# The mixed part of a graph-network kernel with the next graph's preparation first, tags in the matmul weights and interleaved VectorE chains

## What is computed

```python
neigh = (adj_ > 0) & ~eye                      # 512 x 512 per graph
rank = jnp.cumsum(ni, axis=-1) - ni            # which neighbour of the row is it
nb = ni.sum(-1)
skip = where(nb > 10, (nb + 1) // 2, 1)
rem = neigh & (skip > 1) & (rank % skip == skip - 1) & mask   # neighbours that are dropped
rem = rem | swapaxes(rem, 1, 2)
nd = where(rem, 0, adj_) > 0
s = sort(where(nd[..., None], x[:, None], inf), axis=2)       # per node and channel
nv = nd.sum(2)
for tau, w in ((0.25, 0.25), (0.5, 0.5), (0.75, 0.25)):       # three quantiles of the neighbours
    pos = tau * max(nv - 1, 0); lo, hi, frac = floor(pos), ceil(pos), pos - floor(pos)
    agg += w * (s[lo] + frac * (s[hi] - s[lo]))
y = relu((x + agg) @ W1 + b1) @ W2 + b2
```

## Time and profile before

| | |
|---|---|
| median of 3 runs | 3188.49 us (3183.55 to 3193.7) |
| the profiled execution | 3183.33 us, its span 3181.5 us |
| loop over the graphs | about 525 to 2873 us of the span |
| busy share of the span | DVE 88%, PE 70%, ACT 62% |
| mean granted TensorE clock | 0.818 |

### The profile page before, as it was taken

How to read it: one execution, slowest core, us unless ns; L and a number is a source line. 1 busy time by engine, 2 the same in 40 slices (tenths; PEclk the granted TensorE clock), 3 DMA queues, 4 the chain that set the end, 5 groups by cost and what they waited for, 6 DMA issues and landing times.

```text
span 3181.5 us, 45583 instructions
## 1 busy us (share of the span) xinstructions
PE 2234.6 (70%) x16081; PEld 1004.7 (32%) x16234; DVE 2805.6 (88%) x5398; ACT 1987.2 (62%) x3077; POOL 12.4 (0%) x24
## 2 busy tenths in 40 slices
PE   0000014387888888898888888888898889776996
PEld 0000002232333333333333333333333333225664
DVE  7999998999989999999999999999999999546776
ACT  2111443178887878787788787778788777741322
POOL 0000000000000000000000000000000000000000
PEclk6555557688989989898999989899999989886777
DMA  3001000000101001010100101010100100000101
GB/s 68 0 0 26 31 0 0 22 15 20 38 7 35 12 29 26 17 33 12 36 11 31 21 21 34 11 38 8 34 13 29 34 10 19 10 20 27 40 26 40
DMA packets 126916, 72.05 MB, mean 23 GB/s; under 512 B 95513, under 2 KB 110059, under 8 KB 126699
## 3 DMA queue, kind: packets, MB, share of 16 engines
q1 hardware_dynamic: 122570, 68.23, 8.4%
q10 hardware_dynamic: 4128, 1.05, 0.2%
HBM read 41.05 MB, written 15.58 MB: 18 GB/s over the span
## 4 chain that ended last, share of the span: by engine, by line
DVE 57%; PE 27%; ACT 8%; issue 6%; SPq 1%; DMA 1%; DVEq 0%; ACTq 0%
PE ring L624 5%; DVE picked L1527 5%; PE rows L665 4%; ACT hot L1078 3%; PE found_bank L677 3%; PE bcast L637 3%; DVE picked L1519 3%; DVE picked L1511 3%; DVE picked L1521 3%; DVE picked L1493 3%; DVE keys L1329 3%; DVE keys L1330 3%; PE bank L919 2%; DVE picked L1499 2%; DVE delta L1370 2%
## 5 line engine op out<-in xcount | busy, mean ns | idle before, releaser
L1078 ACT ACTIVATE hot<-bcast,consts 128x1024 f16<-128x1024 f32 x744 | 831.5, 1118 | 112.8 <-PE bcast L637 112.8
L624 PE MATMUL ring<-member,neigh_t 128*128 128x512 bf16 x1925 | 495.4, 396 | 40.8 <-issue 16.0
L665 PE MATMUL rows<-hot,table 128*64 128x512 f16 x3072 | 515.8, 416 | 0.0
L1071 ACT ACTIVATE prod<-rows 128x512 f32<-128x512 f32 x720 | 432.1, 600 | 10.1 <-PE rows L665 10.1
L637 PE MATMUL bcast<-idx_t,consts 32*128 32x512 f16 x1488 | 309.5, 413 | 169.4 <-ACT hot L1078 167.6
L654 PE MATMUL rows<-fine_rows,consts 32*128 32x512 bf16 x768 | 314.2, 409 | 18.1 <-DMA fine_rows<-turned 18.0
L624 PEld LDWEIGHTS ring<-member,neigh_t 128*128 128x128 bf16 x2048 | 189.3, 102 | 325.0 <-issue 110.0
L562 PE MATMUL ring<-identb,adj_b 128*128 128x128 bf16 x256 | 33.2, 294 | 358.7 <-ACT adj_b L974 347.3
L677 PE MATMUL found_bank<-prod,consts 128*32 128x512 f32 x1536 | 233.1, 683 | 11.2 <-ACT prod L1071 10.4
L637 PEld LDWEIGHTS bcast<-idx_t,consts 32*128 32x128 f16 x1488 | 70.6, 92 | 510.7 <-ACT hot L1078 338.0
L1527 DVE TENSOR_TENSOR picked<-picked 128x3072 uint16<-128x3072 uint16 (+2 forms) x192 | 209.5, 1091 | 11.2
(11 more groups left out here) (347 smaller groups left out, 4324.7 us busy)
## 6 DMA issues: line engine op xcount, KB each, us to landing
late<-in_adj_dram SPq DMA_DIRECT2D x16, 1024.0 KB, 5.4
adjt_d<-neigh_t SPq DMA_DIRECT2D x16, 512.0 KB, 2.7
fine_rows<-turned SPq DMA_DIRECT2D x512, 8.0 KB
fine_rows<-turned SPq DMA_DIRECT2D x512, 16.0 KB
turned<-adjt_d SPq DMA_DIRECT2D x16, 512.0 KB, 3.6
adj_s<-adjt_d SPq DMA_DIRECT2D x16, 512.0 KB, 4.0
xt_d<-keys SPq DMA_DIRECT2D x2, 1024.0 KB, 10.4
parts_d<-parts SPq DMA_DIRECT2D x4, 512.0 KB, 6.9
```

The source lines that it names most:

```text
L624: ins = mm(ring[u % 2][:, :], kept_t[:, j, P * i:P * i + P], member[:, j, n // 2, 512 * (n % 2):512 * (n % 2) + 512], start=(j == 0), stop ...
L665: ins = mm(rows[u % 2][C * h:C * h + C, :], table[:, s, GROUPS * h + g8, :], hot[:, u % HOT, h, :], start=False, stop=(s == 1), skip_group ...
L1071: run(prod[:, u % DEEP, :], rows[u % 2][:, :], ACT.Relu).then_inc(S["prod_by_act"], 1)
L1078: run(hot[:, u % HOT].rearrange(flat), spread_bank(l, u)[0][:, 0:2, :].rearrange(flat), ACT.Relu, bias=eq_bias[:, :]).then_inc(S["hot_read ...
```

## The change

- On DVE the mixed part is a new function `ahead`. The pieces of the preparation and of the dense layers are now generators, and `beside` puts one of their instructions between two dependent instructions of the search chains. `clear_own` moves ahead of the second `pop`. `gcn_middle` and the drops stand inside the two `narrow`.
- `drop` is one `tensor_scalar` comparison instead of a `scalar_tensor_tensor` with the adjacency. For that, PE adds in each `count_up` one matmul of the adjacency with 4096 on the diagonal (`fence`), and the bias of `apart_from` is lowered by as much.
- The product with the group tag leaves DVE: PE's `sum_first` multiplies by 15 weights `tagged[:, g]` instead of by the identity.
- PE and ACT have new places for their calls: two to five lookups earlier for the preparation of graph p, two lookups instead of one between two pairs of `chunk(p, 0, n)`.
- The last two rounds have functions of their own, `last_region` on PE and ACT and `behind` on DVE.

Of the diff below the calls `count_neighbours` to `count_kept` are those of PE's `region`, `last_region` is PE's too (ACT's has the same form), and `ahead` is DVE's. In `ahead`, the iterators `ranks`, `ffn`, `start`, `middle` and `other` are handed over with `alone`, which issues what is left of one: `ranks` is `rank_bits(p)` and `members(p, 0)`, `ffn` is `ffn_end(d)`, `start` is `gcn_start(d)`, `middle` is `middles(p)`, and `other` is in turn `gcn_middle(d)` with the drops 0 and 1, the drops 2 and 3, and `members(p, 2)`.

```diff
             def count_up(b, i):
+                mm(ring[i % 2][:, :], fence[:, :], adj_b[:, i, :], start=True, stop=False)
                 for j in range(NT):
-                    ins = mm(ring[i % 2][:, P * j:N], ..., start=(j == 0), stop=(j == NT - 1))
+                    ins = mm(ring[i % 2][:, P * j:N], ..., start=False, stop=(j == NT - 1))
...
             def drop(b, i):
-                stt(out=drop1[:, i, :], in0=apart_of[:, i % 2, :], scalar=s2[:, i:i + 1], in1=adj_b[:, i, :], op0=ALU.is_equal, op1=ALU.mult)
+                ts(drop1[:, i, :], apart_of[:, i % 2, :], s2[:, i:i + 1], None, ALU.is_equal)
...
+            def beside(ins, other):
+                n = did(ins)
+                next(other, None)
+                need(n)
...
             def select(b, i, l):
-                tt(first_at[:, 0:last], first[:, C:], first_tag[:, 1:, :].rearrange(flat), ALU.mult).then_inc(S["tile_read"], 1)
-                tt(starts[:, :, 0:last], starts[:, :, 0:last], first_at[:, 0:last]..., ALU.mult)
+                tt(starts[:, :, 0:last], starts[:, :, 0:last], first[:, C:]..., ALU.mult)
...
             def region(t, p, l, d):
-                units(l, STEP[5])
+                units(l, LATE + 5)
                 count_neighbours(p)
+                units(l, LATE + 6)
                 dense_turn(d)
-                units(l, STEP[6])
+                units(l, LATE + 7)
                 count_up(p, 0); count_up(p, 1); dense_third(d)
-                units(l, STEP[7])
+                units(l, LATE + 8)
                 count_up(p, 2)
+                units(l, LATE + 9)
                 count_up(p, 3)
-                units(l, STEP[8]); dense_last(d)
-                units(l, STEP[9])
+                units(l, LATE + 11)
                 both_ways(p, 0); both_ways(p, 1)
-                units(l, STEP[10])
+                units(l, LATE + 12)
                 both_ways(p, 2); both_ways(p, 3)
+                dense_last(d)
-                units(l, STEP[12])
+                units(l, LATE + 15)
                 count_kept(p)
...
+            def last_region(l, d):
+                units(l, 2)
+                dense_first(d)
+                units(l, 6)
+                dense_second(d)
+                units(l, 16)
+                dense_turn(d)
+                units(l, 20)
+                dense_third(d)
+                units(l, 26)
+                dense_last(d)
+                units(l, UNITS)
...
+            def ahead(t_of, p, d):
+                bits_start(t_of, ranks)
+                pop(wl, x2, x4, x8, t, ranks)
+                alone(ranks)
+                bits_first(ffn)
+                alone(ffn)
+                clear_own(p)
+                pop(wl, x2, x4, x8, t, start)
+                alone(start)
+                bits_second(middle)
+                alone(middle)
+                alone(members(p, 1))
+                narrow(x4, 4, other)
+                alone(other)
+                narrow(x2, 2, other)
+                alone(other)
+                bits_last(other)
...
```

More of the change, by code:

```diff
@@ L1180, in region @@
                         chunk(p, 0, n + 1)
+                    if n == 4 and d is not None:
+                        root_of(d, 2)
                 units(l, UNITS + 2)
@@ L1270, in then, with alone, pause @@
                 need(did(ins))
+            def beside(ins, other):
+                n = did(ins)
+                next(other, None)
+                need(n)
+            def alone(other):
+                for _ in other:
+                    pass
+            def pause(n):
+                for _ in range(n):
+                    yield
+            nothing = iter(())
             def restart():
@@ L1594, in bits_first @@
+                stays = did(ts(step, bit, 0.0, None, ALU.is_equal))
+                beside(tt(r, r, t, ALU.subtract), other)
+                flags = did(ts(t.bitcast(I16), bit, -1.0, None, ALU.mult))
+                a_made = did(tt(a_of, blk, bit, ALU.add))
+                need(stays)
                 did(tt(upper_half, wh, step, ALU.mult))
-                then(tt(t, t, mixed, ALU.bitwise_and))
-                then(tt(wl, wl, t, ALU.bitwise_xor))
+                need(flags)
+                beside(tt(t, t, mixed, ALU.bitwise_and), other)
@@ new lines, in drops @@
+            def drops(b, lo, hi):
+                for i in range(lo, hi):
+                    drop(b, i)
+                    yield
+            def ahead(t_of, p, d):
+                ranks = chain(rank_bits(p), members(p, 0)) if p is not None else nothing
+                ffn = chain(degree(d), ffn_end(d)) if d is not None else nothing
+                need(count[0])
+                dve.wait_ge(S["sums_ev"], 2 * (NT * t_of + NT))
+                bits_start(t_of, ranks)
[3 more added lines that the diff above has]
+                alone(ffn)
+                start = chain(pause(2), gcn_start(d)) if d is not None else nothing
```

584 lines of the change are left out of this document (322 added, 262 removed).

## The result

The changed kernel takes 3298.14 us (median; 3292.89 to 3299.85). Beside it the kernel before took 3186.14 us. The ratio is 1.0345, interval 1.0322 to 1.0367: **slower by 3.5%**, some 112 us. The forecast was 3228 with a range up to 3255. The direction was right; the time lies above the range.

A forecast was written before the change was run, and what follows sets the result against it. It took PE, ACT and DVE as a ring of mutual waits, no engine full. 3183.3 - 9.0 - 1.5 + 31 + 2 + 17 = 3223, with the median 5.2 higher 3228 us; range 3140 to 3255.

The forecast's parts named there:

- What bounds the kernel: PE, ACT and DVE wait for each other; less DVE work shortens a period by at most some 3.7 us.
- the ring's floor of 137.8 us: Period of 141.5 us less PE's 3.7 us of waits for DVE: what PE's and ACT's own lists need.
- Tags, drops, interleaving: DVE's list per graph: tags 2.8 us, drops 1.7, interleaving 4.5 to 5 (0.11 a gap); graph 0 gains 9.0.
- The new wait at `clear_own`, and ACT at the third `apart_from`: Middle graphs: DVE waits 2.6 us for the adjacency store; ACT waits 1.8 to 4.7 us for the first drop.
- The step that failed: Third `apart_from` to `turn_idx`: 34.0 us plus 8.0 and 0.7; mixed part 73.7 us for 71.3, +2.4 per graph.
- My upper bound, +3.6 per graph: Middle graphs, if `dense_last` behind `both_ways` were wholly exposed: +3.6 us instead of +2.4.
- Each middle period alike: One period's +2.4 us was applied to all 13 middle graphs: +31 us.
- Graphs 1 and 15: Graph 1 has no dense layers: 0; graph 15 prepares nothing and PE reaches `dense_turn` before DVE: +2 us.
- The last lookups: `dense_first`, now behind unit 1, waits for the transposed features; fourteen units run after it: +17 us (+10 to +22).
- Freed engines: DVE's gain comes ahead of PE's and ACT's waits, so 3.66 us go per middle graph: 3149 us; chance 0.24.
- No gain from interleaving: An operation between two dependent DVE ones saves nothing, so 2.5 us return per middle graph: 3266 us; chance 0.05.

The follow-up runs named there:

- tags: Kernel before with the group tags in PE's weights alone, the product gone from DVE; 3147 us, ratio 0.9874.
- tf: Kernel before with both `tags` and `fence`; 3142 us, ratio 0.9856.
- places2: Changed kernel with PE's and ACT's `region` calls at the old places, but ACT's `root_of(d, 2)` behind the chunks 6 and 7; 3166 us, ratio 0.9930.
- apart4: Changed kernel with four `apart_of` buffers instead of two, so no `apart_from` waits for a drop; 3260 us, ratio 1.0238.
- front2: `places2` with `count_neighbours`, `dense_turn`, ACT's answering calls, the four `count_up` and four `apart_from` at the new places; 3267 us, ratio 1.0252.
- space: Changed kernel with `chunk(p, 0, n)` at the old places, one lookup between pairs; 3282 us, ratio 1.0307.
- tail14: Changed kernel with `dense_first` to `dense_last` of the last rounds 14 to 20 lookups later; 3290 us, ratio 1.0333.
- chained: Changed kernel with each inserted DVE instruction issued behind the wait of the dependent pair instead of between; 3328 us, ratio 1.0440.
- fence: Kernel before with the fence matmul and the single-comparison drops alone; 3179 us, ratio 0.9980.
- places: Changed kernel with PE's and ACT's calls in `region` at the old places; 3270 us, ratio 1.0262.

## Why the prediction was off

- **What bounds the kernel.** Right. DVE's busy share was no bound: 10 us less work per period gave nothing by itself, and the ring's floor of 137.8 us shows in `tags`, `tf` and `places2` (means of 138.4 to 139.1).
- **Tags, drops, interleaving.** Right in size, but for graph 0. Two drops take 0.62 us where they took 1.42 (forecast 0.25 each), the weights cost nothing. Without the interleaving the middle periods are 2.5 us longer in the mean, as put down for it, but graph 0 only 2.3 us, for 5. Up to the first `turn_idx` the whole gave -11.8 for -10.5.
- **The new wait at `clear_own`, and ACT at the third `apart_from`.** Right to 0.2 us, and `apart4` confirms it as a cause: 34 us.
- **The step that failed**: the stretch behind ACT's third `apart_from`, put at the old 34.0 us, 8.0 for five more units and 0.7 for `dense_last`. It gave 42.7 us, measured were 46.4. ACT's work there grew by 7.9 us, as costed. But its idle time from the third `apart_from` on, summed over the brackets in its timeline, is 9.8 us where 5.3 had stood in the kernel before: +4.5 instead of +0.7. I had carried over an old stretch whole, with PE and ACT overlapping in it as they did. Now each engine in turn waits for the other (1.48 and 3.08 us on ACT, 0.65 to 1.79 us ahead of most spreads on PE). Why is known in part only. That the later calls stand closer together can't be all of it: in `front2` they are spread as before, and ACT still idles 9.0 us there. What `front2`, `space` and the changed kernel share is the third `apart_from` five units earlier, with its wait. The place of the low clock, for which the prediction had no term, has a share. From the granted clock it covers 3.4 of the old 34.0 us, 6.5 of the 46.4 and 13.7 of the 45.6 in `front2`; by the three rows under `front2` I estimate 1.2 us of the 4.5 for it in the changed kernel. How the rest divides stays open. My upper bound, +3.6 per graph, came from `dense_last` alone and was too low.
- **Each middle period alike.** Wrong. I costed one period, and five of the 13 are longer by another 3 us (149.7 to 150.2). The same code runs in periods of 146.8 to 152.5 us in `tail14`. The rows show what differs between two periods of the changed kernel: PE's low-clock stretches lie elsewhere. In the stretch behind the third `apart_from` it is 0.89 in a long period and 0.93 in a short one, and that stretch takes 47.9 us for 46.4, half of the difference. What decides where they lie I have not settled. It makes some 15 us here.
- **Graphs 1 and 15**: +5.7 and +5.2 for 0 and +2. In graph 1 ACT waits for DVE 2.77 us at the first `apart_from` and 1.06 at the third. In graph 15 ACT idles 5 us more, spread over many rows; which call brings it is open.
- **The last lookups**: right, +21.4 for +17 with the wait of 41 us as described.
- **The rivals.** "Freed engines" was the case of `places2` (3166) and not of this kernel. "No gain from interleaving" fell with `chained`. The Trainium skill ("VectorE: DVE Perf Modes", section "The DRAIN you can't avoid") has it that the next operation doesn't start until the pipeline is empty. The same section adds that one that isn't held starts earlier, which the prediction left out when it put the term at zero by the page. The rows above fit this addition: a small independent operation in between started 0.28 us behind the first and cost nothing. I had no rival that was slower by more lost overlap, and the range ended at 3255 for want of it.

## What to carry to other kernels

Before work is moved ahead in one engine's list, ask whom the moved call waits for: an early call with a gate that doesn't move (here a DMA and a double buffer) turns slack into a wait, and everything that was queued behind it pays. When two engines answer each other call by call, a stretch's length is not its old length plus the work added; the idle time of both has to be laid out again for the new order. Take the parts of a change that only remove work (`tags`, `fence`: -1.4%) apart from the parts that move it, and measure them alone.

## What the runs showed of the hardware

- A wait can cost more than its length. In `places` ACT waits 4.7 us for a root, and PE 3.95; the eight chunk matmuls behind it run at a granted clock of 0.50 and take 3.59 us instead of 1.90. The periods are 8.1 us longer in the mean than in `places2`, for the place of that one call.
- The mean clock over a period doesn't tell what the low clock costs. In the kernel before a period at 0.92 took 141.5 us and one at 0.91 took 140.2. In the stretch behind the third `apart_from` it is 32.7 us at 1.00 and 35.4 at 0.90.
- A short DVE operation put between two dependent ones of 128x768 started 0.28 us behind the first and left the second's start at 0.38 us (0.39 with nothing between).
- A weight that is the same for 15 matmuls was loaded 15 times (98 ns each), so that 15 different ones cost the same.
- A comparison of 128x512 from 16-bit input against a scalar takes 0.353 us on DVE, by the changed kernel's group (shortest, median and longest in ns); the two-operation form with a third tensor took 0.747 in the kernel before.

```profile
L1448 DVE SCALAR_TENSOR_TENSOR adj_b<-apart_of,small,adj_b x64: 743/747/753, 418.2 to 2584.5; 128x512 bf16<-128x512 f16 x64
```

```profile
L1540 DVE TENSOR_SCALAR adj_b<-apart_of,small x64: 346/353/356, 418.5 to 2656.4; 128x512 bf16<-128x512 f16 x64
```
